# First loads and projections in the order in which they are needed, and low weight parts one slot behind the high ones

## What is computed

```python
def reference(x, ctx, ...):
    # attention: 16 query heads, 4 key/value heads of 128, rotary q and k, causal
    q, k = rope(x @ Wq + bq), rope(x @ Wk + bk); v = x @ Wv + bv
    wei = softmax(mask(q @ k.T / sqrt(16)))
    x = layernorm(x + (wei @ v) @ Wo + bo)
    # a recurrence over the 256 tokens in each channel, with decay w and bonus u
    x = layernorm(x + wkv(w, u, x, ctx))
    # a dense layer plus 16 low-rank experts of rank 16, the best two of a router
    h = silu(x @ rw1.T + rb1); coeff = top2_softmax(h @ rw2.T + rb2 + gates)
    return layernorm(x @ W.T + bias + sum_e coeff_e * (x @ A_e.T) @ B_e.T)
```

## Time and profile before

| | |
|---|---|
| Median of 3 runs | 1627.79 us (1626.96 to 1629.46) |
| Profiled execution | 1626.13 us, span 1624.3 us |
| Mean granted TensorE clock | 0.988 |
| PE busy | 1545.0 us (95%) |
| DVE, ACT, POOL busy | 82%, 69%, 62% |
| DMA | 202.60 MB, mean 125 GB/s |

### The profile page before, as it was taken

One profiled execution on the slowest core, in us unless ns is written; L12 is line 12 of the kernel. 1 busy time (PEld: TensorE's weight loads), 2 busy tenths in 40 slices (PEclk: granted clock), 3 DMA queues, 4 the chain that ended last, 5 costly groups with the idle time before them and its releaser, 6 DMA issues.

```text
span 1624.3 us, 32607 instructions
## 1 busy us (share of the span) xinstructions
PE 1545.0 (95%) x10464; PEld 1400.8 (86%) x10464; DVE 1329.1 (82%) x3428; ACT 1115.3 (69%) x2979; POOL 1011.6 (62%) x855
## 2 busy tenths in 40 slices
PE   5899999999999999999999999999999977989997
PEld 4799999999999999999999999999999966768885
DVE  4666688898988898988898989888989885967864
ACT  4778777878787878787878787878787764334332
POOL 3455576666666766667666666676667632735652
PEclk9999999999999999999999999999999998999999
DMA  7766444424442444244424442444244412122211
GB/s 236 232 207 230 135 134 150 140 60 145 154 138 60 147 151 139 60 142 155 140 60 149 148 140 59 142 155 140 60 141 152 147 49 88 53 83 74 78 65 52
DMA packets 83144, 202.60 MB, mean 125 GB/s; under 512 B 11808, under 2 KB 12832, under 8 KB 82976
## 3 DMA queue, kind: packets, MB, share of 16 engines
q1 hardware_dynamic: 82976, 200.53, 39.6%
HBM read 120.80 MB, written 37.75 MB: 98 GB/s over the span
## 4 chain that ended last, share of the span: by engine, by line
PE 76%; DVE 12%; issue 5%; ACT 3%; POOL 2%; DVEq 1%; SPq 1%; DMA 0%; ACTq 0%; POOLq 0%
PE bank L507 23%; PE bank L508 22%; PE bank L509 22%; PE bank L621 5%; PE bank L543 2%; DVE PS L1238 1%; DVE RC L1114 1%; PE bank L604 1%; PE bank L612 1%; PE bank L544 1%; DVE QS L1231 1%; ACT Xh L709 1%; DVE OTl L1154 1%; DVE ED L1249 1%; DVE SW L1302 1%
## 5 line engine op out<-in xcount | busy, mean ns | idle before, releaser
L507 PE MATMUL bank<-Xh,W 128*128 128x256 f32 x1280 | 361.8, 283 | 25.4 <-DVE RC L1114 15.4
L509 PE MATMUL bank<-Xh,W 128*128 128x256 f32 x1280 | 359.5, 281 | 0.0
L508 PE MATMUL bank<-Xl,W 128*128 128x256 f32 x1280 | 359.2, 281 | 0.0
L973 POOL TENSOR_TENSOR Ql<-RC,Qh 128x512 fp32r<-128x512 f32 x128 | 171.3, 1338 | 213.8 <-ACT Qh L709 213.8
L724 ACT ACTIVATE S<-S,NM 128x128 f32<-128x128 f32 (+1 forms) x512 | 228.1, 447 | 77.0 <-DVE NM L1099 76.1
L507 PEld LDWEIGHTS bank<-Xh,W 128*128 128x128 f32 x1280 | 243.9, 191 | 29.4 <-DVE RC L1114 11.2
L509 PEld LDWEIGHTS bank<-Xh,W 128*128 128x128 f32 x1280 | 244.0, 191 | 0.0
L508 PEld LDWEIGHTS bank<-Xl,W 128*128 128x128 f32 x1280 | 243.1, 190 | 0.0
L963 POOL TENSOR_TENSOR SW<-SW,tables 128x512 f32<-128x512 f32 x128 | 168.1, 1313 | 119.8 <-DMA SW<-QB 119.7
L709 ACT ACTIVATE S<-S,RL 128x128 f32<-128x128 f32 (+1 forms) x512 | 203.9, 448 | 48.0 <-DVE RL L1106 46.5
L709 ACT ACTIVATE PTh<-bank 128x384 fp32r<-128x384 f32 x256 | 124.9, 488 | 151.1 <-PE bank L621 150.1
(11 more groups left out here) (152 smaller groups left out, 4406.6 us busy)
## 6 DMA issues: line engine op xcount, KB each, us to landing
W<-kept SPq DMA_DIRECT2D x140, 512.0 KB, 4.4
SW<-QB SPq DMA_DIRECT2D x256, 128.0 KB, 2.3
kept<-W SPq DMA_DIRECT2D x40, 512.0 KB, 4.7
XR<-in_xt SPq DMA_DIRECT2D x16, 512.0 KB, 4.3
XR<-XR SPq DMA_DIRECT2D x64, 128.0 KB, 2.4
RO<-in_xn SPq DMA_DIRECT2D x16, 512.0 KB, 3.9
KVT<-in_ctxt SPq DMA_DIRECT2D x16, 512.0 KB, 4.2
mixed<-RO SPq DMA_DIRECT2D x16, 512.0 KB, 4.0
```

Of the source, the lines that this page charges most:

```text
L507: nc.tensor.matmul(dst, lhs[0], rhs[0], start=first, stop=False)
L508: nc.tensor.matmul(dst, lhs[0], rhs[1], start=False, stop=False)
L509: return nc.tensor.matmul(dst, lhs[1], rhs[0], start=False, stop=last)
L973: gp.tensor_tensor(Q[1][:, :, :], RC[:, i % 2, :, :], Q[0][:, :, :], ALU.subtract).then_inc(q_lo, 1)
```

## The change

The first pieces are loaded and split in a new order (`FIRST_ORDER`: K, K, Q0, Q1, V, V, Q2 ...), and V of position 0 is projected in slots 1 and 2, in slot 2 ahead of the q projection. x of batch 1 has a buffer of its own (a part of RO) and is loaded among the first pieces; its high part is made in slot -5 and its low part in slot -4. The high part of an x is made in two instructions, and the low parts of batches 0 and 1 on VectorE alone. The high part of the first K moves from slot 0 to slot 3, and its low part to VectorE. The constants come in three transfers, bo in a fourth in slot 1, and two pieces (the ninth and tenth) are asked for behind the first K swap. VectorE makes the low parts of pieces due in slot 0 or later one slot after their high parts; pieces are asked for 3 slots ahead, and none of the later ones before slot 1. In the router a drain takes the place of a semaphore. Semaphore counts are adapted.

```diff
+FIRST_SPLIT, FIRST_V, SECOND_X = 3, [1, 2], -5
+FIRST_ORDER = [PK, PK + 1, PQ, PQ + 1, PV, PV + 1] + list(range(PQ + 2, NP))
-SPLIT_AT = [[-7, -6, -5, -5, -3, -2, -2, -1, 0, 1, 2, 3] + [h // 2 + 4 for h in range(HEADS)],
+SPLIT_AT = [[-6, -6, -2, -2, -6, -6, 0, 1, 1, 2, 3, 4] + [h // 2 + 4 for h in range(HEADS)],
...
-AHEAD = 4
+AHEAD = 3
...
+FIRST_LOAD = 1
...
+def nth_piece(hf, i):
+    return hf * NP + (i if hf else FIRST_ORDER.index(i))
+def x_pos(n, m):
+    s = 1 if n == SECOND_X + m - 1 else next_pos(n, m)
+    return None if s == 1 and n != SECOND_X + m - 1 else s
+def split_pos(n):
+    s = 0 if n == FIRST_SPLIT else next_pos(n, K_SPLIT)
+    return None if s == 0 and n != FIRST_SPLIT else s
...
+    if n in FIRST_V:
+        return "V", FIRST_V.index(n), 0
...
+    units = [("Q", n, 0)] * (n >= 0) + [extra_of(n)] * (extra_of(n) is not None)
+    UNITS += units[::-1] if n == FIRST_V[1] else units
...
+        X1R = RO[:, 3, :, :].rearrange("p a c -> p (a c)").rearrange("p (k t) -> p k t", k=KC)
...
-        def run(eng, slot, splits=None, ffn_weights=None, step=None, ahead=0):
+        def run(eng, slot, splits=None, ffn_weights=None, step=None, ahead=0, behind=0):
...
-                        for i in range(NP):
-                            if SPLIT_AT[hf][i] - ahead == n:
+                        for i in range(NP) if hf else FIRST_ORDER:
+                            if n == (max(SPLIT_AT[hf][i] - ahead, FIRST_LOAD) if ahead else SPLIT_AT[hf][i] + behind * (SPLIT_AT[hf][i] >= 0)):
                                 splits(hf, i)
...
                     sp.dma_start(KSW[64:128, :, :], KB[0:64, :, :]).then_inc(k_swapped, 16)
+                    if s == 0:
+                        for u in range(8, STAGES):
+                            load_piece(u)
...
-                if s is not None and x_first(s + 1) is not None:
+                if s is not None and s > 0 and x_first(s + 1) is not None:
...
+                if n == 1:
+                    sp.dma_start(Bo[:, :], bo).then_inc(const_more, 16)
...
-            load_piece(PK)
-            load_piece(PK + 1)
-            for dst, src in FIRST_CONSTS:
-                load_const(dst, src, const_first)
-            for i in range(4):
-                load_piece(PV + i)
-            for dst, src in CONSTS:
-                load_const(dst, src, const_in)
-            for u in range(PV + 4, STAGES):
+            load_piece(0)
+            load_piece(1)
+            sp.dma_start(smalls[:, :], small).then_inc(const_first, 16)
+            sp.dma_start(tables[:, 0:2 * T], trig_t).then_inc(const_first, 16)
+            load_piece(2)
+            load_piece(3)
+            load_x(1)
+            for u in range(4, 8):
                 load_piece(u)
-            for dst, src in MORE:
-                load_const(dst, src, const_more)
+            sp.dma_start(late[:, TT * C - P - T:TT * C + P], late_t).then_inc(const_in, 16)
...
+                if n == FIRST_V[1]:
+                    extra(n)
+                    heads_q(n)
+                else:
+                    heads_q(n)
+                    extra(n)
...
+                    for h in range(2):
+                        copy(two(X[0][:, XBUF[s], :, :], h), two(x_raw(b), h)).then_inc(x_hi, 1)
...
-                copy(X[0][:, XBUF[s], :, :], XR[:, :, :]).then_inc(x_hi, 1)
...
+                    for h in range((b > 1)):
+                        gp.tensor_tensor(two(X[1][:, XBUF[s], :, :], h), two(x_raw(b), h), two(X[0][:, XBUF[s], :, :], h), ALU.subtract).then_inc(x_lo, 1)
...
+            def first_k_low(n):
+                if split_pos(n) == 0:
+                    dve.wait_ge(k_hi, 1)
+                    v.tensor_tensor(K[1][:, 0, :, :], KRC[:, :, :], K[0][:, 0, :, :], ALU.subtract).then_inc(k_lo, 1)
...
+                    for h in range((b > 1), 2):
+                        dve.wait_ge(x_hi, 2 * b + h + 1)
+                        v.tensor_tensor(two(X[1][:, XBUF[s], :, :], h), two(x_raw(b), h), two(X[0][:, XBUF[s], :, :], h), ALU.subtract).then_inc(x_lo, 1)
...
-                        v.tensor_scalar(SE, EM, 1.0, None, ALU.add).then_inc(top_sum, 1)
-                        dve.wait_ge(top_sum, f + 1)
+                        v.tensor_scalar(SE, EM, 1.0, None, ALU.add)
+                        dve.drain()
...
-            run(dve, slot, splits, ffn_weights, step)
+            run(dve, slot, splits, ffn_weights, step, behind=1)
```

More of the change, by code:

```diff
@@ L465, in load_piece @@
                     sp.wait_ge(w_lo, u - STAGES + 1)
-                sp.dma_start(stages[u % STAGES], wraw[u // NP, u % NP, :, :]).then_inc(stage_in[u % STAGES // 2], 16)
-            def load_const(dst, src, done):
-                sp.dma_start(dst[tuple(slice(None) for _ in dst.shape)], src).then_inc(done, 16)
+                piece = FIRST_ORDER[u] if u < NP else u - NP
+                sp.dma_start(stages[u % STAGES], wraw[u // NP, piece, :, :]).then_inc(stage_in[u % STAGES // 2], 16)
             def splits(hf, i):
-                if hf * NP + i >= STAGES:
-                    load_piece(hf * NP + i)
+                if nth_piece(hf, i) >= STAGES:
+                    load_piece(nth_piece(hf, i))
             def ffn_weights(n):
@@ L531, in bank_free, with extra, heads_q @@
                         pe.wait_ge(x2_sum, TT * k + tt + 1)
+            def extra(n):
+                e = extra_of(n)
+                if e:
+                    kind, tile, s = e
+                    proj_free(*e)
+                    if kind == "K":
+                        if tile == 0:
+                            pe.wait_ge(x_lo, 2 * SEQ[s][1] + 2)
+                        piece_loaded(s, PK + tile)
+                        for kc in range(KC):
+                            last = three(proj_ps(*e), [wk_tile(i, tile, kc) for i in range(2)],
+                                         [x[:, XBUF[s], kc, :] for x in X], kc == 0, kc == KC - 1)
+                        last.then_inc(k_projected, 1)
+                    else:
+                        if tile == 0:
+                            piece_loaded(s, PV)
+                            piece_loaded(s, PV + 1)
+                        for kc in range(KC):
+                            last = three(proj_ps(*e), [x[:, XBUF[s], kc, tile * P:(tile + 1) * P] for x in X],
+                                         [wv_tile(i, kc) for i in range(2)], kc == 0, kc == KC - 1)
+                        last.then_inc(v_projected, 1)
+            def heads_q(n):
+                g = head_of(n, 0)
+                if g is not None:
+                    s = g // HEADS
+                    m = g % HEADS
+                    piece_loaded(s, PQ + m)
+                    proj_free("Q", g, 0)
+                    for kc in range(KC):
+                        last = three(proj_ps("Q", g, 0), [wq_tile(i, m, kc) for i in range(2)],
+                                     [x[:, XBUF[s], kc, :] for x in X], kc == 0, kc == KC - 1)
+                    last.then_inc(q_projected, 1)
             def slot(n):
-                m = n % HEADS
                 g = head_of(n, L_S)
@@ L760, in even, with x_high, extras @@
                     copy(K[0][:, s % 2, :, :], KRC[:, :, :]).then_inc(k_hi, 1)
+            def x_high(n):
+                s = x_pos(n, 1)
+                if s is not None and x_first(s) is not None:
+                    b = x_first(s)
+                    act.wait_ge(x1_in if b == 1 else x_in, 16 if b < 2 else 16 * b)
+                    if b >= 2:
+                        act.wait_ge(q_projected, n - 1)
+                    for h in range(2):
+                        copy(two(X[0][:, XBUF[s], :, :], h), two(x_raw(b), h)).then_inc(x_hi, 1)
+            def extras(n):
+                e = extra_of(n)
+                if e:
+                    kind, tile, s = e
+                    if kind == "K":
+                        act.wait_ge(k_projected, JL * s + tile + 1)
+                        above(act, k_swapped, 32 * s)
+                        if s == 0 and tile == 0:
+                            act.wait_ge(const_first, 32)
+                        nc.scalar.activation(KB[:, tile, :], proj_ps(*e), ACT.Identity,
+                                             bias=Bk[:, SEQ[s][0], tile:tile + 1]).then_inc(k_biased, 1)
+                    else:
+                        act.wait_ge(v_projected, TT * s + tile + 1)
+                        above(act, mixed_v, HEADS // 2 * (s - 1))
+                        copy(V[0][:, s % 2, tile, :], proj_ps(*e)).then_inc(v_hi, 1)
+            def even(n):
+                split_k(n)
                 tail(n, 0)
@@ L779, in odd @@
                 before_rotation(n)
[L780 to L794, removed]
-                if s is not None and x_first(s) is not None:
-                    b = x_first(s)
-                    act.wait_ge(x_in, 16 * b + 16)
-                    if b >= 2:
-                        act.wait_ge(q_projected, n - 1)
-                    copy(X[0][:, XBUF[s], :, :], XR[:, :, :]).then_inc(x_hi, 1)
```

(12 more changed lines are left out.)

117 lines of the change are left out of this document (61 added, 56 removed).

## The result

| | before | after |
|---|---|---|
| Median of the fast runs (6 and 7) | 1627.38 us | 1620.68 us |
| Ratio, with its 95% interval | | 0.996 (0.9947 to 0.9972) |
| Profiled execution, span | 1624.3 us | 1617.5 us |
| First matmul | 8.21 us | 7.19 us |
| First score (head 0, slot 4) | 33.65 us | 26.23 us |

A forecast was written before the change was run, and what follows sets the result against it. TensorE was taken to bound the kernel from 68.68 us on, so gains lie before that: 9.2 + 5.5 - 0.2 = 14.5 us, giving 1613.3 us. The range was 1607 to 1622.

The forecast's parts named there:

- Start: Before the first matmul: split x copies and VectorE low parts move it from 8.21 to 7.5 us, 0.7 us.
- To the first score: From kernel start to head 0's score in slot 4: reordered units bring it 9.2 us earlier, ends 6 and 10.1.
- the walk: Unit-by-unit timing up to the first score, without collisions: score near 23.6 us, 10.1 us earlier.
- The stall of ScalarE for pieces 8 and 9: Slots 1 to 2: ScalarE waits to 18.4 us for Q4's late piece, so Q3 starts 1.6 us late.
- Slots 4 to 9: First score to head 6's score: low parts one slot later end VectorE's waits, 5.5 us, between 0 and 10.0.
- Rival D: First score no earlier, held by SyncE's or ScalarE's order in slots 1 to 3; about 1627 us, chance 0.08.
- Steady stretch: Slots 10 to 27: VectorE's waits vanish beside a full TensorE; gain at most 1.0 us, taken as nothing.
- The time after head 6's score is not the same as before: Sign of being wrong: the forecast needs the time from head 6's score (slot 10) on unchanged.
- Tail: Last stage, router: a drain replaces a semaphore wait 16 times; loss taken as 0.2 us, 1.4 at worst.
- A: Slots 4 to 9 keep 35.03 us, set by ScalarE's high parts and its waits; 1618.8 us, chance 0.16.
- C: Crowded DMA queue makes swaps and pieces land late, so the kernel is slower; 1632.6 us, chance 0.06.

## Why the prediction was right in sign and wrong in size

**Start.** Forecast 7.5 us for the first matmul, measured 7.19. Right in mechanism, 0.3 us better.

**To the first score.** Forecast 9.2 us with 10.1 by the walk; measured 33.65 - 26.23 = 7.4. ScalarE starts writing QB of head 1 at 15.19 us, near the 14.9 of the walk. The stall of ScalarE for pieces 8 and 9 was not there: it makes Q4's high part at 17.64 us without a wait. What came instead is VectorE beside GpSimd: two low parts in slot 2 took 1.45 and 1.75 us and not 0.7 each (of the kernel after):

```profile
17.77 1.45 DVE L1405 TENSOR_TENSOR W<-E2Z,W 128x512 fp32r<-128x512 f32 x1
19.15 1.75 DVE L1405 TENSOR_TENSOR W<-ED,W 128x512 fp32r<-128x512 f32 x1
20.83 0.47 DVE L1162 SCALAR_TENSOR_TENSOR RC<-bank,smalls,tables 128x256 f32<-128x256 f32 x1
```

TensorE then idled for 2.13 us up to 21.78, and ran the next units at the low clock (0.50 granted, the 1.2 GHz level), at 0.41 us for a matmul that takes 0.28 at the full clock. The rows for the stretched operations were in rows 4, but I took only 0.9 us for them. The larger part is the clock, which the walk left out. With 128 unused bytes in the changed kernel the same two low parts took 1.42 and 1.79 us and TensorE idled for 2.10, yet the clock stayed up, and the first score came at 24.43 us, the 9.2 us of the forecast. From 22 to 24 us, the kernel after first, then that with 128 bytes:

```profile
22.00:24.00 2.00, 2.00 (x11) 2.00 (x11) 1.19 (x2) 0.63 (x1) 1.26 (x2) 0.50 0.99 369
22.00:24.00 2.00, 2.00 (x19) 2.00 (x18) 1.19 (x3) 0.88 (x2) 1.51 (x1) 1.00 0.97 352
```

All nine profiled executions with both parts of the change divide so: with the low clock the first score came at 26.23 to 26.85 us (four), with the full clock at 24.05 to 24.92 (five). What decides between the two is open.

**Slots 4 to 9.** Forecast 5.5 us, measured 35.03 - 29.18 = 5.9. Right in size. But the parts were credited wrongly. The order of loads, which had 9.2 us in my sum, gives nothing without the slot behind; the slot behind alone brings the first score 1.6 us earlier and shrinks slots 4 to 9 by 6.3 us. Rival D's first score, no earlier than before, is what that order gives alone (33.42 us), but not by D's causes: ScalarE waited only 1.9 us there for weights, and what holds is VectorE's wait in the same slot. For the change as a whole D does not hold.

**Steady stretch, the step that failed.** The prediction says that "whatever starts earlier simply ends earlier", and takes "nothing" for the steady stretch. Both first terms came nearly whole: 13.3 us at head 6's score, where 14.7 were forecast. Had the rest been as before, the time would have been near 1614.5. Instead 7.1 us are lost in pace between pairs 28 and 124 alone, and the step that failed is this term put at nothing. I costed the instructions of the change and not the memory that they use: the small constants gathered into `smalls` made the space ahead of x larger by 448 bytes, which the new kernel's buffers show. With x at the distance 128 instead of 192 from W, each q and K projection matmul takes 2 ns longer. "The time after head 6's score is not the same as before" was named as a sign of being wrong, and it came: 1562.1 us of the span instead of 1555.6. The kernel with 64 unused bytes is the test of the rest of the sum: 1609.8 us against 1626.2, a gain of 16.4 where the sum said 14.5. Of it 14.2 us are there at head 6's score, where the sum had 14.7; the other 2 are mostly in the last stage and are not explained.

**Tail.** In the first router step the drain leaves 0.07 us before the next instruction and the semaphore left 0.04. Over all 16 steps this idle time is 1.5 us against 0.6, a loss of 0.9 where I took 0.2; it does not show in the end, since the stage from the last pair on took 303.2 us instead of 303.9.

**Rivals.** A's time (1618.8) is nearest to the measurement but its mechanism is not there: the slots did shrink. C was seen in a small part: the swap of heads 4 and 5 took up to 4.9 us to land in the kernel after, and taking the copies out of its way gained nothing. The range from 1607 to 1622 held the time, but by luck: its upper part was there for a gain of only 6 us up to the first score, not for a loss behind head 6's score.

## What to carry to other kernels

When a change adds, drops or resizes a buffer, compare the addresses of the matmul operands before and after, and try a few dozen unused bytes: in this kernel, which TensorE bounds, 64 such bytes were worth more than the change without them (10.1 us against 6.7), and they can hide a gain or pass for one. Test such an edit with the old distances restored before judging the rest. And an engine that works through a list in order should not wait for another engine's work of the same slot ahead of work that the bounding engine needs; the same new order of loads gave nothing with that wait in place and some 4.9 us without it.

## What was not expected of the hardware

A 256-column matmul of the q and K projections (x by weights) took 279 to 284 ns by the distance between its two operands in SBUF modulo 256 bytes, at a granted clock of 1.00: in its first pass 280 at distance 192, 281 at 64 and 160, 282 at 128 and 224, 284 at 0. The whole kernel was 10.1 us slower at 128 than at 192, of which 7.0 in the stretch where TensorE is full, and 14.1 us slower at 0 than at 192 with all buffers moved (11.0 with x alone). Moving both operands together left the pace as it was (981.3 against 980.5 to 981.6 us). Why the distance matters, whether 256 is its true period, and how much the probabilities and head outputs add stays open; no run took these apart. The ends of matmuls in a trace are modelled, so the 2 ns are to be read with the pace, which is taken from starts on GpSimd.
